# Batch 0's first two layer-0 tiles in plain float32, with the startup loads in another order

## The reference

```python
x = x + (x @ W.T + (x @ lora_A[label]) @ lora_B.T * 0.5)     # layer 0, label per batch
x = x + quantise(x, thresholds, deltas, zeropoints)          # layer 1: 8 groups by |x|
x = x + x @ weight[adapter].T                                # layer 2, adapter per batch
x = x + (x @ B[adapter].T) @ A[adapter].T                    # layer 3, rank 16
```

## Time and profile before

| | |
|---|---|
| median of 3 runs | 464.24 us |
| the profiled execution | 464.56 us |
| its span, first to last instruction | 462.7 us |
| TensorE busy | 454.7 us |
| VectorE busy | 415.4 us |
| ScalarE busy | 326.7 us |
| bytes moved | 69.15 MB |

### The profile page before, as it was taken

One profiled execution on the slowest core, in us unless ns is written; L12 is line 12 of the kernel. 1 busy time (PEld: TensorE's weight loads), 2 busy tenths in 40 slices (PEclk: granted clock), 3 DMA queues, 4 the chain that ended last, 5 costly groups with the idle time before them and its releaser, 6 DMA issues.

```text
span 462.7 us, 7306 instructions
## 1 busy us (share of the span) xinstructions
PE 454.7 (98%) x3006; PEld 410.9 (89%) x3006; DVE 415.4 (90%) x395; ACT 326.7 (71%) x274; POOL 8.1 (2%) x18
## 2 busy tenths in 40 slices
PE   7999999999999999999999999999999999999995
PEld 7899999889998899889998899989998899988884
DVE  4889999999699996999699996999869999999983
ACT  5699979958398747967398754996349848665730
POOL 1000000000000000000000000100000000000000
PEclk9999999999999999999999999999999999999999
DMA  7983430557128534367227543183322522245242
GB/s 279 343 334 104 91 103 1 91 188 279 69 92 221 196 142 159 69 204 279 76 91 188 197 174 126 48 261 132 120 92 91 181 92 96 75 173 180 94 159 91
DMA packets 17941, 69.15 MB, mean 149 GB/s; under 512 B 2421, under 2 KB 3445, under 8 KB 13045
## 3 DMA queue, kind: packets, MB, share of 16 engines
q1 hardware_dynamic: 17044, 62.41, 37.5%
q0 software_dynamic: 864, 6.29, 7.3%
HBM read 54.01 MB, written 8.39 MB: 135 GB/s over the span
## 4 chain that ended last, share of the span: by engine, by line
PE 90%; DMA 3%; issue 2%; DVE 2%; SPq 2%; ACT 1%; DVEq 0%; ACTq 0%
PE l_ps L838 39%; PE l_ps L773 37%; PE l_ps L853 6%; PE bx_ps L872 2%; PE l_ps L783 2%; DMA w_sb<-w 2%; PE bx_ps L799 2%; DMA adapter_ids<-adapters 1%; PE l_ps L902 1%; PE bx_ps L806 1%; PE bx_ps L879 1%; DVE quant L628 1%; ACT cand L439 0%; ACT magnitude L429 0%; SPq L287 0%
## 5 line engine op out<-in xcount | busy, mean ns | idle before, releaser
L838 PE MATMUL l_ps<-x,w_sb 128*128 128x256 f32 x896 | 196.9, 380 | 0.4 <-DVE x L595 0.4
L838 PEld LDWEIGHTS l_ps<-x,w_sb 128*128 128x128 f32 x896 | 169.2, 190 | 25.3 <-issue 2.8
L634 DVE COPY_PREDICATED quant<-mask,cand 128x2048 f32<-128x2048 int8 (+2 forms) x77 | 145.6, 1891 | 0.4
L439 ACT ACTIVATE cand<-x,inv_delta 128x2048 f32<-128x2048 f32 (+2 forms) x88 | 134.5, 1528 | 8.8 <-DVE quant L628 7.0
L449 ACT ACTIVATE mask<-magnitude,thr_bias 128x2048 fp8e5<-128x2048 f32 (+2 forms) x77 | 117.7, 1529 | 13.4 <-DVE quant L634 12.7
L608 DVE TENSOR_SCALAR cand<-cand,delta 128x2048 f32<-128x2048 f32 (+2 forms) x88 | 87.9, 999 | 10.1 <-ACT cand L439 9.8
L616 DVE TENSOR_SCALAR cand<-cand,lower,upper 128x2048 f32<-128x2048 f32 (+2 forms) x88 | 93.4, 1062 | 0.4
L773 PE MATMUL l_ps<-x_hi,w_hi 128*128 128x256 f32 x512 | 87.1, 292 | 0.9 <-DVE x_lo L565 0.9
L773 PE MATMUL l_ps<-x_hi,w_lo 128*128 128x256 f32 x512 | 82.8, 283 | 0.0
L773 PE MATMUL l_ps<-x_lo,w_hi 128*128 128x256 f32 x512 | 82.5, 283 | 0.0
L773 PEld LDWEIGHTS l_ps<-x_hi,w_hi 128*128 128x128 f32 x512 | 71.4, 191 | 6.6 <-issue 4.2
(11 more groups left out here) (66 smaller groups left out, 231.0 us busy)
## 6 DMA issues: line engine op xcount, KB each, us to landing
w_sb<-w SPq DMA_DIRECT2D x31, 1024.0 KB, 4.9
out<-x SPq DMA_DIRECT2D x32, 256.0 KB, 2.2
x_raw<-x SPq DMA_DIRECT2D x15, 512.0 KB, 6.4
x_lo<-x_raw POOLq DMA_DIRECT2D x6, 1024.0 KB, 8.2
a_raw<-a SPq DMA_DIRECT2D x8, 512.0 KB, 3.6
w_sb<-w SPq DMA_DIRECT2D x7, 512.0 KB, 7.4
b_sb<-b SPq DMA_DIRECT2D x8, 256.0 KB, 2.7
a_raw<-a SPq DMA_DIRECT2D x8, 128.0 KB, 6.3
```

What stands on the lines that cost most here:

```text
L439: act.activation(cand[:, c % CANDS, 0:n], x2_unit(u), ACT.Identity, bias=ROUND, scale=inv_delta[:, k:k + 1]).then_inc(rounded, 1)
L634: dve.copy_predicated(y, mask[:, m % MASKS, 0:n].bitcast(I8), t).then_inc(merged, 1)
L838: last = nc.tensor.matmul(l2_bank(b, q)[:, i * S:(i + 1) * S], w2_tile(b, o)[:, k * P:(k + 1) * P], x2[:, b % SLOTS, k * S:(k + 1) * S], s ...
```

## The change

- The first two tiles (n = 0 and 1, outputs 0 and 2) of batch 0 are no longer split products but plain float32 ones on the staged weights and on `x_raw` (`plain0`, `first_tiles`). They go by pieces as these land: quarters of x and halves of the two tiles, which are now loaded in turn.
- The high and low parts of tiles 0 and 1, which batches 1 to 7 use, are made after those of tile 7, ahead of `drain_l0(0, 0)` on ScalarE and of the quantisation on VectorE. The tile that is split in two halves is now tile 2.
- Tiles 6 and 7 are staged in `x3`, without a wait; layer 2's first quarters wait for other counts.
- a0's load moves ahead of tiles 3 and 4, which come after the wait for the ids; the id lists move ahead of the second tile's first half.
- VectorE's `split_w0(5)` moves ahead of `add_diag(6)`. The warm-up is 10 products and not 14.

```diff
-WARM = 14
+WARM = 10
         def w0_stage(n):
-            return w2_sb[:, n // 2 % CHUNKS, n % 2, :]
+            if n >= 2 * CHUNKS:
+                return x3[:, n % 2 * T * P:(n % 2 + 1) * T * P]
+            return w2_sb[:, n // 2, n % 2, :]
         def w0_pieces(n):
-            return n + 2
+            return (n + 6) % T + 2
             def load_w0(n):
-                if n >= 2 * CHUNKS:
-                    sp.wait_ge(w0_split_done, w0_pieces(n - 2 * CHUNKS))
                 sp.dma_start(w0_stage(n), w0[ORDER[n]]).then_inc(w0_loaded[n], 16)
             def load_w2(b, q, adapter):
-                        sp.wait_ge(w0_split_done, w0_pieces((7, 3, 5)[q]))
+                        sp.wait_ge(w0_split_done, w0_pieces(2 * q + 1))
# SP, the start
+            load_first_x(0, x_quarter_loaded[0])
+            load_first_w0(0, 0, w0_half_loaded[0])
+            load_first_x(1, x_loaded[0])
             sp.dma_start(label_ids[:, :], ...)
             sp.dma_start(adapter_ids[:, :], ...)
-            for n in range(1, 5):
-                load_w0(n)
+            load_first_w0(1, 0, w0_half_loaded[1])
+            load_first_x(2, x_quarter_loaded[1])
+            load_first_w0(0, 1, w0_loaded[0])
+            load_first_x(3, x_loaded[1])
+            load_first_w0(1, 1, w0_loaded[1])
+            load_w0(2)
             sp.wait_ge(ids_loaded, 2 * 16)
             load_a0(0)
+            load_w0(3)
+            load_w0(4)
# ScalarE
-            for h in range(2):
-                split_first_x(h)
-                split_first_w0(h)
-            split_first_x(2)
-            split_first_x(3)
-            for n in range(1, 5):
-                split_w0(n)
+            for h in range(4):
+                split_first_x(h)
+            for h in range(2):
+                split_first_w0(h)          # tile 2 now
+            split_w0(3)
+            split_w0(4)
...
             split_w0(6)
             split_w0(7)
+            split_w0(0)
+            split_w0(1)
             drain_l0(0, 0)
# VectorE
+            add_diag(0)
             split_first_x(0)
-            add_diag(0)
-            split_first_w0(0)
-            split_first_x(1)
-            split_first_w0(1)
-            split_first_x(2)
-            add_diag(1)
-            split_first_x(3)
-            add_diag(2)
-            split_w0(1)
-            add_diag(3)
-            split_w0(2)
+            add_diag(1)
+            for h in range(1, 4):
+                split_first_x(h)
+            add_diag(2)
+            split_first_w0(0)
+            add_diag(3)
+            split_first_w0(1)
+            split_w0(3)
             add_diag(4)
-            split_w0(3)
             split_w0(4)
             add_diag(5)
...
+            split_w0(5)
             add_diag(6)
-            split_w0(5)
...
             split_w0(6)
             split_w0(7)
+            split_w0(0)
+            split_w0(1)
# TensorE
+            def plain0(n, k, start=False):
+                o = ORDER[n]
+                if k == o:
+                    pe.wait_ge(diag_added, n + 1)
+                nc.tensor.matmul(l0_ps[:, 0, o * S:(o + 1) * S], w0_stage(n)[:, k * P:(k + 1) * P],
+                                 x_raw[:, k * S:(k + 1) * S], start=start, stop=False)
+            def first_tiles():
+                pe.wait_ge(x_quarter_loaded[0], 16)
+                pe.wait_ge(w0_half_loaded[0], 16)
+                plain0(0, 1, start=True)
+                plain0(0, 0)
+                pe.wait_ge(x_loaded[0], 16)
+                plain0(0, 2)
+                plain0(0, 3)
+                pe.wait_ge(w0_half_loaded[1], 16)
+                plain0(1, 0, start=True)
+                ...                        # (1, 1), (1, 3), (1, 2); then x quarter 2 and w0[0]: (0, 4), (0, 5);
+                ...                        # x's last quarter: (0, 6), (0, 7); w0[1]: (1, 4) to (1, 7)
             def tile0(n):
-                main0(b, o)
+                if n == 0:
+                    first_tiles()
+                elif n > 1:
+                    main0(b, o)
```

More of the change, by code:

```diff
@@ L112, in build @@
         x_loaded = [sem(f"x_loaded{h}") for h in range(2)]
-        x_quarter_loaded = sem("x_quarter_loaded")
-        w0_half_loaded = sem("w0_half_loaded")
+        x_quarter_loaded = [sem(f"x_quarter_loaded{h}") for h in range(2)]
+        w0_half_loaded = [sem(f"w0_half_loaded{n}") for n in range(2)]
         a0_loaded = sem("a0_loaded")
@@ L348, in split_w0 @@
                 act.wait_ge(diag_added, n + 1)
+                if n < 2:
+                    act.wait_ge(w0_loaded[n], 16)
                 act.activation(w0_hi[:, ORDER[n], :], w0_stage(n), ACT.Copy).then_inc(w0_hi_done, 1)
@@ L352, in split_first_w0 @@
                 cols = slice(h * CW, (h + 1) * CW)
[L353 to L357 removed]
+                act.wait_ge(diag_added, 3)
+                act.activation(w0_hi[:, ORDER[2], cols], w0_stage(2)[:, cols], ACT.Copy).then_inc(w0_hi_done, 1)
             def split_first_x(h):
                 cols = slice(h * CW, (h + 1) * CW)
[L361 removed]
+                act.wait_ge((x_quarter_loaded[0], x_loaded[0], x_quarter_loaded[1], x_loaded[1])[h], 16)
                 act.activation(x_hi[:, 0, cols], x_raw[:, cols], ACT.Copy).then_inc(x_hi_done, 1)
@@ L542, in add_diag @@
                 o = ORDER[n]
-                if n == 0:
-                    dve.wait_ge(w0_half_loaded, 16)
+                if n < 2:
+                    dve.wait_ge(w0_half_loaded[n], 16)
                 else:
@@ L558, in split_first_w0 @@
                 dve.wait_ge(w0_hi_done, h + 1)
-                dve.tensor_tensor(w0_lo[:, 0, cols], w0_stage(0)[:, cols], w0_hi[:, 0, cols].bitcast(F32),
+                o = ORDER[2]
+                dve.tensor_tensor(w0_lo[:, o, cols], w0_stage(2)[:, cols], w0_hi[:, o, cols].bitcast(F32),
                                   ALU.subtract).then_inc(w0_split_done, 1)
@@ L755, in main0 @@
                     pe.wait_ge(x0_done, 2 * (b - 1) + h + 1)
-                parts = ((0, 2), (2, 4), (4, 6), (6, 8)) if b == 0 and o == 0 else ((0, 4), (4, 8))
-                for first, end in parts:
-                    if b == 0 and o == 0:
-                        pe.wait_ge(w0_hi_done, 1 if first < HALF else 2)
-                        pe.wait_ge(x_split_done, (first + 2) // 2)
-                    elif b == 0:
+                for first, end in ((0, HALF), (HALF, T)):
+                    if b == 0:
+                        pe.wait_ge(x_split_done, 4)
+                        pe.wait_ge(w0_hi_done, 1 if n == 2 and first == 0 else w0_pieces(n))
+                    elif b == 1 and n < 2:
                         pe.wait_ge(w0_hi_done, w0_pieces(n))
-                    elif o == 0 and b < ADDED:
+                    if o == 0 and 0 < b < ADDED:
                         pe.wait_ge(x_split_done, x_pieces(b, first // HALF))
-                    elif o == 0:
+                    elif o == 0 and b >= ADDED:
                         pe.wait_ge(x_added, 16 * (b - ADDED + 1))
                     for w, v in ((w0_hi, x_hi), (w0_hi, x_lo), (w0_lo, x_hi)):
-                        if b == 0 and w is w0_lo:
-                            pe.wait_ge(w0_split_done, w0_pieces(n) if o > 0 or first >= HALF else 1)
+                        if w is w0_lo and b == 0:
+                            pe.wait_ge(w0_split_done, 1 if n == 2 and first == 0 else w0_pieces(n))
+                        elif w is w0_lo and b == 1 and n < 2:
+                            pe.wait_ge(w0_split_done, w0_pieces(n))
                         for k in range(first, end):
@@ L774, in main0 @@
                                              start=(o % 2 == 0 and v is x_hi and w is w0_hi and k == 0), stop=False)
+            def plain0(n, k, start=False):
[14 more added lines that the diff above has]
+                plain0(1, 0, start=True)
+                plain0(1, 1)
+                plain0(1, 3)
+                plain0(1, 2)
+                pe.wait_ge(w0_loaded[0], 16)
+                pe.wait_ge(x_quarter_loaded[1], 16)
+                plain0(0, 4)
+                plain0(0, 5)
+                pe.wait_ge(x_loaded[1], 16)
+                plain0(0, 6)
+                plain0(0, 7)
+                pe.wait_ge(w0_loaded[1], 16)
+                for k in range(HALF, T):
+                    plain0(1, k)
             def close0(b, o):
```

19 lines of the change are left out of this document (6 added, 13 removed).

## The result

The changed kernel takes 466.88 us (median of 6 runs, 465.98 to 467.29), the kernel before 464.29 us beside it (6 runs, 464.09 to 465.04). The ratio is 1.0052, 95% interval [1.0039, 1.0065]: slower by 2.4 us by the ratio (2.6 by the medians), where 464.5 and "no change" had been forecast, in a range of 463.7 to 465.6. The profiled execution took 466.47 us with a span of 464.7.

The account below looks back on a forecast made before the run. TensorE, busy 98% of 462.7 us, was taken as the bound. Its lead of 2.5 us less 1.4, 0.65, 0.25, 0.2 and 0.3 gave -0.3, so 464.5 us in the median's terms, range 463.7 to 465.6.

Parts of the forecast that it names:

- The plain tiles and the warm-up: TensorE's start: plain products run from about 5.9 to 13.3 us without a gap, no load waited for; lead 2.5 us.
- rival 3: Plain products: clock stays at 1.2 GHz up to 9 us, ending 1 us later; same time, counted within the forecast's 0.72.
- (a): Batch 0's sum_low: TensorE waits for drain_low behind b0's split, b0 landing at 17.2 again; 1.4 us of lead lost.
- (b): Batch 0's closing products: wait for low_rank_lo(0), at 22.5 instead of 22.98 through the swap on VectorE; 0.65 us lost.
- (c): Start of VectorE's chain to the closes: tile 5's diagonal slips by 0 to 0.5 us, taken as 0.25 us lost.
- The bill on VectorE and ScalarE: Splits of tiles 0 and 1 ahead of batch 0's quantisation: that chain starts 1.7 us later.
- the forecast waits of 0.2 and 0.3 us: TensorE at tile 8 (x's low part) and batch 1's close (low_rank_lo(1)): later by 0.2 and 0.3 us.
- SP's two waits, load_w2 and x2: Two removed SP waits, load_w2 of quarter 0 about 2 us later, x2 with 4.1 us of margin: no cost.
- Rival 2: Late loads: tile 3 issued at 9.8 behind the ids, b0 and tiles 5, 7 a microsecond late; 465.5 us, chance 0.15.
- Its sign: What would show late loads: any stretch before 20 us in which the DMA share falls well under 1.
- Rival 1: The lead is kept: 461.7 us, or 463.3 if loads come a microsecond earlier; together chance 0.10.
- The rule of the skill: Early loads: 2.0 us plus bytes at 436 GB/s puts tile 6 in by 15.1 us, where the trace has 20.88.

Follow-up runs that it names:

- e11: The kernel before, with b0 laid out four times over and loaded by one copy into all 128 partitions; its time moved by 0.36 us, before 464.28 us.
- e13: The changed kernel with b0 laid out four times over and loaded by one copy into all 128 partitions; 464.96 us, before 464.28 us.
- e4: The changed kernel with the id lists moved back and tiles 3 and 4 issued before the wait for the ids; 466.29 us, ratio to before 1.0049.
- e9: The kernel before, with x's second half and tile 1 each loaded in two pieces with 2 KB rows; 464.49 us, ratio to before 1.0017.
- e1: The changed kernel with 12 more identity products before sum_low, to keep TensorE busy in its wait; 465.88 us, ratio to before 1.0032.
- e5: The kernel before, with two more passes each on ScalarE and VectorE ahead of the quantisation; 464.66 us, ratio to before 1.0006.
- e3: The changed kernel with drain_low(0) ahead of b0's split and the first four tiles closed after tile 4; 467.78 us, ratio to before 1.0064.

## Why the prediction was wrong, step by step

- **The plain tiles and the warm-up: right.** They run from 5.96 to 13.2 without a gap (forecast 5.9 to 13.3), at a clock of 1.00 from 7.30 on, so rival 3 did not happen. The loads they need came up to 0.9 us later than forecast (x's third quarter at 8.7 and not 7.8), and still none was waited for.
- **(a) is the step that failed:** "The bytes ahead of b0 in the queue are the same in the new order, so b0 lands at 17.2 again." It landed at 18.7. The bytes are the same, the pace is not: b0's narrow copies slow what flies with them, and in the new order more of the other loads' packets do (at least 136 slow ones against at least 62). The prediction had seen that b0 goes in narrow pieces, and let it be since "the change leaves those as they are"; it leaves the copies, but issues them at 8.2 to 9.8 us, 0.6 us behind tile 4, where they had been issued at 9.7 to 11.1, 4.3 us behind it. With one wide copy b0 comes 1.7 us earlier in the kernel before (17.20 to 15.52) and 2.7 in the changed one (18.73 to 16.06), so 1.0 of the 1.5 us of lateness comes from the narrow copies. The other 0.5 is still there between e11 and e13, and tile 2 is late by about as much (11.4 to 12.0), which is what the slower queue of 5.0 to 8.5 us leaves behind. Why it is slower there stays open: e4, with the id lists moved back, has most of the busy share again (0.97) but not the rate; e9's smaller pieces make tile 2 0.3 us late, but not b0. The times leave 0.7 us between e13 and the kernel before.
- **The clock was not in the sum.** The wait of 1.4 us was priced as itself; at 2.91 us it was followed by 3.5 us at a clock of 0.51, which cost another 0.9 to 1.0 us (e1 against the changed kernel, by their times). In the trace: sum_low and tile 3 take 25.08 - 20.23 = 4.85 us in place of 0.43 + 2.87 = 3.30; the 1.2 of it that lies past 23.89 (`low_rank_lo` done at 23.84, and a hand-over of 0.05) is lost.
- **(b) was right in its own term, not in who waits last.** `low_rank_lo` came at 23.84 and not 22.5, because its chain starts with b0 and tile 5; from tile 5's diagonal to its end the chain took 3.90 us in place of 4.45, so the swap saved 0.55 where 0.45 was forecast. But in the changed kernel TensorE didn't wait for it: tile 3 at the low clock ended later. The forecast wait shows in e1 (0.35) and e13 (0.60). Against the 22.98 of before that is 0.9 us; with the 1.2 of the clock, the 2.1 by which the closes are later (25.08), and 2.0 at batch 0's layer 2.
- **(c)** was taken as 0.25 us: the diagonal of tile 5 was to slip to 18.7, by VectorE and ScalarE taking tiles 3 and 4 in turn, and slipped to 19.94, where tile 5's own load ended the wait. In e13, where that load is in at 17.5, the turn-taking is what is left, and the diagonal starts at 18.65.
- **The bill on VectorE and ScalarE: right in place, too small by 1.1 us.** The chain came 2.83 us later, not 1.7. But TensorE itself was 2.0 later, so the margins are 1.7 - 2.83 + 2.01 = 0.9 and 1.39 - 2.83 + 2.01 = 0.6, as the rows show, and nothing waited: the forecast waits of 0.2 and 0.3 us did not happen, as TensorE's own loss covered them. e5, where only the lateness stands, has tile 8 0.16 us later and batch 1's close 0.30, near the forecast 0.2 and 0.3; e3, with the lead kept, shows 3.12.
- **SP's two waits, load_w2 and x2:** no cost, as forecast; no gap of TensorE behind 24 us but the 0.4 that stood before as well.
- **The rivals.** Rival 2 had the right side and half of the size (b0 and tile 5 a microsecond late). Its sign, a stretch before 20 us in which the DMA share falls well under 1, is there (0.87 from 5.0 to 8.5), but its mechanism is not: it needed tile 3 issued at 9.8 behind the ids, and tile 3 was issued at 6.9. That stretch goes with the 0.5 us that stays open, and not with b0's copies, in whose stretch the share is 1.07 (13.5 to 16.5). Rival 1's condition, loads a microsecond earlier, was met in e13 (b0 at 16.1, tile 5 at 17.5), and the lead was still eaten by ScalarE's and VectorE's order: 464.96, and not 463.3.
- **The rule of the skill.** The section "Anatomy of one DMA" of the Trainium skill's page "DMA: Bandwidth & Descriptors" is on DMAs that GpSimd issues, and SyncE issues these loads. The trace doesn't agree with the 15.1 us: tile 6 landed at 20.9 before and at 21.3 after. The reason that the prediction gave for it, b0's narrow pieces, is worth only 0.8 us of that (tile 6 at 20.1 in e11).

With b0 out of the way (e13: gap 1.74 to 18.84, forecast 1.4 to 18.6; closes at 22.98, forecast 22.5; tile 8 waiting 0.55, forecast 0.2) the sum of the prediction comes out within 0.5 us of its 464.5. Its term (c) describes e13, and (b) and the wait at tile 8 do within 0.5 us. That (a) fits is in part luck: it had b0's split start when b0 lands, at 17.2; in e13 b0 is in at 16.1, and the split starts at 17.39, behind ScalarE's pass over tile 4, which VectorE held up. The changed kernel differs from e13 by b0's copies: 466.88 - 464.96 = 1.9 us by the medians, of a loss of 2.6.
